# Twenty-eight tiles' experts chosen at the head of one step, the router's gap behind the k transposes, and one power of two columns

## The reference

```python
x = x + xattn(layernorm(x), ctx, ctx, Wq, bq, ..., Wo, bo)   # 16 heads of 32, 77 context tokens, causal mask
x = x + ffn(layernorm(x), ...)

# ffn(hidden), hidden read as S = 8, B = 512: attention runs over the 8 sequences
ln1 = layer_norm(hidden) * ln1_w + ln1_b
q, k, v = split(ln1 @ qkv.T)                   # 16 query heads, 4 k/v heads, causal over S
h1  = hidden + softmax(q k / sqrt(32)) v @ proj.T
ln2 = layer_norm(h1) * ln2_w + ln2_b
top_p, top_i = top_k(softmax(ln2 @ router), 2) # 8 experts, 2 per token, shares sum to 1
# tokens of each expert in order of their number, at most 1280 per expert
fc1 = gelu(tokens @ w1[e]);  fc2 = fc1 @ w2[e]
out = h1 + sum over the token's experts of share * fc2
```

## Time and profile before

| | us |
|---|---|
| median of 3 runs (lowest to highest) | 1679.21 (1679.16 to 1680.63) |
| profiled execution | 1678.78 |
| its span, first to last instruction | 1677.0 |
| PE busy in the span | 1520.7 (91%) |
| PEld, DVE, ACT, POOL busy | 1325.8, 951.9, 713.4, 837.0 |
| PE, DVE, POOL busy from 330 to 640 | 304.0, 226.5, 185.5 of 310 |
| PE, DVE, POOL busy from 850 to 900 | 21.9, 29.2, 11.8 of 50 |
| PE busy from 1000 to 1677 | 637.7 of 677 |

### The profile page before, as it was taken

The page is one execution under the profiler, slowest core; times in us unless marked ns, Lnnn a source line. Parts: engine busy times, 40 slices in busy tenths (PEclk is TensorE's granted clock), DMA queues, the critical chain, the costliest instruction groups (busy, mean ns, idle before and its releaser), DMA issues. The chain is left out here.

```text
span 1677.0 us, 30921 instructions
## 1 busy us (share of the span) xinstructions
PE 1520.7 (91%) x11103; PEld 1325.8 (79%) x11104; DVE 951.9 (57%) x1780; ACT 713.4 (43%) x1448; POOL 837.0 (50%) x953
## 2 busy tenths in 40 slices
PE   7788788999999999998863999899999979999986
PEld 5566677888888888877752989899999869899975
DVE  4766656777777767677756445543233555343361
ACT  2343443555554455455435434433332534343341
POOL 1343444556655556678741637453343665463242
PEclk9999889999999999999975999999999989999999
DMA  6111211122222212222211424343442533442221
GB/s 240 39 51 58 70 51 51 46 76 77 71 67 67 66 63 72 69 95 79 80 57 55 102 57 105 75 110 68 90 89 41 110 98 76 97 102 51 36 40 23
DMA packets 63597, 124.58 MB, mean 74 GB/s; under 512 B 13232, under 2 KB 13648, under 8 KB 62921
## 3 DMA queue, kind: packets, MB, share of 16 engines
q1 hardware_dynamic: 45184, 92.54, 16.9%
q0 software_dynamic: 17920, 29.31, 10.4%
q10 hardware_dynamic: 328, 0.50, 0.1%
HBM read 89.02 MB, written 46.27 MB: 81 GB/s over the span
## 5 line engine op out<-in xcount | busy, mean ns | idle before, releaser
L1351 PEld LDWEIGHTS hidden_ps<-gT,w 128*128 128x128 f32 x2880 | 350.4, 192 | 9.1 <-ACT hT L1270 4.2
L1351 PE MATMUL hidden_ps<-gT,w 128*128 128x256 f32 x2880 | 352.7, 284 | 5.3 <-ACT hT L1270 3.2
L1380 PE MATMUL expert_ps<-w,hT 128*128 128x512 f32 x1440 | 341.7, 397 | 8.1 <-DVE og L1320 8.1
L1380 PEld LDWEIGHTS expert_ps<-w,hT 128*128 128x128 f32 x1440 | 272.4, 191 | 65.9 <-DVE og L1320 8.5
L1295 DVE TENSOR_TENSOR hT<-gl,hT 128x512 fp32r<-128x512 f32 x160 | 130.5, 824 | 250.4 <-ACT hT L1270 250.3
L1155 POOL TENSOR_TENSOR w<-raw,w 128x1024 fp32r<-128x1024 f32 x64 | 155.0, 2433 | 201.2 <-ACT w L1149 200.8
L1268 ACT ACTIVATE gl<-hidden_ps 128x512 f32<-128x512 f32 x160 | 95.7, 598 | 335.3 <-PE hidden_ps L1351 312.6
L1252 POOL DMA_INDIRECT out_dram<-og,idx x80 | 130.3, 1628 | 153.7 <-DVE og L1320 140.0
L1320 DVE TENSOR_SCALAR og<-expert_ps,kept 128x512 f32<-128x512 f32 x80 | 59.1, 749 | 159.0 <-PE expert_ps L1380 154.9
L1278 ACT ACTIVATE gT<-yk 128x256 fp32r<-128x256 f32 x160 | 66.9, 418 | 109.1 <-DVE yk L1306 107.3
L1024 PE MATMUL main_ps<-wqkv_hi,zT 128*128 128x512 f32 x256 | 109.0, 441 | 4.8 <-DVE h L798 4.8
(11 more groups left out here) (178 smaller groups left out, 3225.6 us busy)
## 6 DMA issues: line engine op xcount, KB each, us to landing
raw<-L_ffn_moe_w_dram SPq DMA_DIRECT2D x64, 512.0 KB, 3.6
normed_tokens<-h SPq DMA_DIRECT2D x128, 65.0 KB
xa<-x_dram SPq DMA_DIRECT2D x32, 256.0 KB, 2.7
xc<-x_dram SPq DMA_DIRECT2D x32, 256.0 KB, 3.0
attended_rows<-x SPq DMA_DIRECT2D x32, 256.0 KB, 2.0
fx<-attended_rows SPq DMA_DIRECT2D x128, 64.0 KB
out_dram<-fx SPq DMA_DIRECT2D x128, 64.0 KB
fx<-qkv_rows_dram SPq DMA_DIRECT2D x1, 1536.0 KB, 6.6
```

The costliest lines, as they stand in the source:

```text
L1351: last = pe.matmul(pH[:, q, f * W:(f + 1) * W], w1[p][l][:, k, cols], xT[g.s % 2][r][:, k, :], start=k == 0 and n == 0, stop=k == KT - 1 a ...
L1380: last = pe.matmul(pY[:, k, :], hT[par][l][:, f, k * P:(k + 1) * P], w2[p][r][:, f, :], start=f == 0 and n == 0, stop=f == FT - 1 and n == 2)
```

## The change

- `CHOICES` has three batches: 28 tiles at step 48, 3 at step 50, the last one behind the loop. A batch is now chosen at the head of its step, ahead of the h addition. The buffer `equal` grows for it.
- MAX8 and gap stand behind the q and k transposes.
- `rff` goes. POOL makes both variances in two columns, one `pow` of two columns gives z's factor and h's, and `rstd_f` comes with that.
- The first expert's pieces are loaded at steps 38, 40, 42, 44, 46, 47, 48 and 49 (`FIRST_PIECES`) and halved one step later.
- `BY_ACT` is 4: VectorE makes four of the eight one-hot rows.
- ScalarE makes `wq_hi` ahead of its four first DMA issues, and the token tables and `wo_hi` in step 2 instead of step 1.

```diff
@@ -51,7 +51,7 @@
 BATCH = 8
-BY_ACT = 6
+BY_ACT = 4
@@ -162,8 +162,9 @@
 LATE = NT + LP + 2
-CHOICES = ((LATE, 0, 9), (LATE + 2, 9, 18), (LATE + 6, 18, 24), (LATE + 10, 24, 28), (STEPS - 2, 28, 31),
-           (STEPS, 31, 32))
+FIRST_PIECES = {LATE: (0,), LATE + 2: (1,), LATE + 4: (2,), LATE + 6: (3,), LATE + 8: (4,), LATE + 9: (5,),
+                LATE + 10: (6,), LATE + 11: (7,)}
+CHOICES = ((STEPS - 4, 0, 28), (STEPS - 2, 28, 31), (STEPS, 31, 32))
@@ -235,7 +236,7 @@
     token_mask = sb("token_mask", [TB, 16 * TB], F32R)
-    expo = sb("expo", [P, 1])
+    expo = sb("expo", [P, 2])
@@ -273,7 +274,7 @@
     wx, wf, wh = sb("wx", [P, 1]), sb("wf", [P, 2]), sb("wh", [P, 1])
-    rx, rf, rff, rh = sb("rx", [P, 2]), sb("rf", [P, 8]), sb("rff", [P, 2]), sb("rh", [P, 2])
+    rx, rf, rh = sb("rx", [P, 2]), sb("rf", [P, 8, 2]), sb("rh", [P, 2])
@@ -421,9 +422,9 @@
                     sp.dma_start(choice["product"][:, 0:3 * P], a["routing_orders"]).then_inc(const_in, 16)
-                if 0 <= i - LATE < CH:
+                for j in FIRST_PIECES.get(i, ()):
                     sp.wait_ge(s["x2_done"], NT)
-                    weights["load"](sp, 0, 0, 0, i - LATE)
+                    weights["load"](sp, 0, 0, 0, j)
@@ -504,13 +505,12 @@
                     var = mvf[:, f % 2, 1:2]
-                    link(pool, "pool_link", linked,
-                         pool.tensor_scalar(wf[:, 0:1], var, 1.0 + EPS, EPS * EPS, ALU.mult, ALU.add))
-                    pool.tensor_tensor(rff[:, f % 2:f % 2 + 1], wf[:, 0:1], expo[:, 0:1], ALU.pow)\
-                        .then_inc(s["rstd_f"], 1)
+                    pool.tensor_scalar(wf[:, 0:1], var, 1.0 + EPS, EPS * EPS, ALU.mult, ALU.add)
+                    link(pool, "pool_link", linked, pool.tensor_scalar(wf[:, 1:2], var, EPS, None, ALU.add))
                     need(pool, s["h0_done"], f - 7)
-                    link(pool, "pool_link", linked, power(rf[:, f % 8:f % 8 + 1], var, wf[:, 1:2]))
-                    pool.tensor_scalar(shift[:, f % 8:f % 8 + 1], mvf[:, f % 2, 0:1], rf[:, f % 8:f % 8 + 1], -1.0,
+                    pool.tensor_tensor(rf[:, f % 8, :], wf[:, :], expo[:, :], ALU.pow).then_inc(s["rstd_f"], 1)
+                    pool.wait_ge(s["rstd_f"], f + 1)
+                    pool.tensor_scalar(shift[:, f % 8:f % 8 + 1], mvf[:, f % 2, 0:1], rf[:, f % 8, 1:2], -1.0,
@@ -523,18 +523,18 @@
                     pool.memset(groups["xg"][:, :, :, :], 0.0).then_inc(s["xg_cleared"], 1)
-                if 0 <= i - LATE - 1 < CH:
-                    weights["low"](pool, 0, 0, i - LATE - 1)
+                for j in FIRST_PIECES.get(i - 1, ()):
+                    weights["low"](pool, 0, 0, j)
             pool.wait_ge(s["xg_cleared"], 1)
 
         @block.scalar
         def _(act):
+            act.wait_ge(wq_in, 16)
+            act.activation(wq[0][:, :, :], rq, ACT.Copy).then_inc(s["wq_hi"], 1)
             act.dma_start(x2[0:TB, 0, 0:P], a["token_sel"]).then_inc(tok_in, 16)
             act.dma_start(x2[0:TB, 1, :], a["token_mask"]).then_inc(tok_in, 16)
             act.dma_start(bv, a["L0_xattn_bv"].partition_broadcast(SK)).then_inc(bias_in, 16)
             act.dma_start(bo[:, :], a["L0_xattn_bo"].partition_broadcast(P)).then_inc(bias_in, 16)
-            act.wait_ge(wq_in, 16)
-            act.activation(wq[0][:, :, :], rq, ACT.Copy).then_inc(s["wq_hi"], 1)
@@ -542,7 +542,7 @@
                         .then_inc(s["xt_hi"], 1)
-                if i == 1:
+                if i == 2:
@@ -588,7 +588,7 @@
                     need(act, s["piece_lo"], 8)
                     act.activation(h1[:, f % 4, 0:D], fx[:, f % FX, :], ACT.Identity, bias=shift[:, f % 8:f % 8 + 1],
-                                   scale=rf[:, f % 8:f % 8 + 1]).then_inc(s["h0_done"], 1)
+                                   scale=rf[:, f % 8, 1:2]).then_inc(s["h0_done"], 1)
@@ -640,8 +640,8 @@
                         .then_inc(s["consts_done"], 1)
-                if 0 <= i - LATE - 1 < CH:
-                    weights["high"](act, 0, 0, i - LATE - 1)
+                for j in FIRST_PIECES.get(i - 1, ()):
+                    weights["high"](act, 0, 0, j)
@@ -791,6 +791,9 @@
                     low_halves(i)
+                batch = chosen(i, 0)
+                if batch is not None:
+                    choose(*batch)
@@ -859,12 +862,6 @@
                     dve.reciprocal(rec2[:, f % 2, :], den2[:, :]).then_inc(s["rec2_done"], 1)
-                f = tile(i, FF + 5)
-                if f is not None:
-                    dve.wait_ge(s["lg_evac"], f + 1)
-                    chained(dve.max(tops[:, f, :], logits[:, f, :]))
-                    need(dve, s["gap_exp"], f)
-                    dve.tensor_tensor(gap[:, :], tops[:, f, 1:2], tops[:, f, 0:1], ALU.subtract).then_inc(s["gap"], 1)
@@ -883,6 +880,12 @@
                     k_turn.then_inc(s["k_turned"], 1)
+                f = tile(i, FF + 5)
+                if f is not None:
+                    dve.wait_ge(s["lg_evac"], f + 1)
+                    chained(dve.max(tops[:, f, :], logits[:, f, :]))
+                    need(dve, s["gap_exp"], f)
+                    dve.tensor_tensor(gap[:, :], tops[:, f, 1:2], tops[:, f, 0:1], ALU.subtract).then_inc(s["gap"], 1)
@@ -904,11 +907,8 @@
                     dve.wait_ge(s["val_mm"], S)
                     need(dve, s["zt_mm"], f)
-                    dve.tensor_scalar(z, fx[:, f % FX, :], mvf[:, f % 2, 0:1], rff[:, f % 2:f % 2 + 1],
+                    dve.tensor_scalar(z, fx[:, f % FX, :], mvf[:, f % 2, 0:1], rf[:, f % 8, 0:1],
                                       ALU.subtract, ALU.mult).then_inc(s["z_done"], 1)
-                batch = chosen(i, 0)
-                if batch is not None:
-                    choose(*batch)
@@ -1081,7 +1081,7 @@
                "is_blk": sb("is_blk", [P, 2, BATCH, NBLK], F16), "hot_blk": sb("hot_blk", [P, 2, BATCH, NBLK], F16),
-               "equal": sb("equal", [P, 9, E]), "hot": sb("hot", [P, 2, NT, E]), "rest": sb("rest", [P, NT, E]),
+               "equal": sb("equal", [P, NT, E]), "hot": sb("hot", [P, 2, NT, E]), "rest": sb("rest", [P, NT, E]),
```

## The result

The changed kernel takes 1716.54 us (median of 4 runs, 1711.17 to 1718.79); the kernel before, run beside it, 1679.92 us (1679.16 to 1681.22). The ratio is 1.0213, with a 95% interval of 1.0187 to 1.0238. Slower was forecast; the size, +17.6 us for a measured +36.6, was wrong, and the time lies outside the range of 1684 to 1711. A second set of five runs of the changed kernel gave 1715.43 us and 1.0206 (1.0188 to 1.0224).

A forecast was written before the change was run, and what follows sets the result against it. Bound: TensorE in full steps, a ring through z in late steps, then a chain without overlap. Sum 11.3 - 0.5 + 2.9 + 3.4 + 3.3 - 4.8 + 0 + 2 = +17.6 on 1678.8: forecast 1696 us, range 1684 to 1711.

The forecast's parts named there:

- Parts 1 and 2, full steps: Steps 20 to 32: late gap and two-column power delay z and xT_lo, +11.3 us; a vanished wait gives -0.5.
- Part 2, steps 13 to 18: Steps without a gap yet: the later power ends before VectorE comes to z, so 0 us.
- Part 3: Late steps: z's chain has no slack, +1.95 us a turn; +5.8 before step 38, -2.9 to 47, together +2.9.
- Clock: Late turns: each leaves TensorE a 2 us hole, after which its clock may be lower; +2 us (0 to 13).
- the clock rival: Lower TensorE clock returns in every late turn: nine of 1.5 us, +13.5 instead of +2, total 1708 us; chance 0.20.
- Part 4: Head of step 48: choosing 28 tiles overruns VectorE's idle time, operations blocked by POOL; +3.4 us (0.2 to 4).
- Part 5: Counts: 84 matmuls instead of 12 before the last tile's router matmul; +3.3 us (+1 to +6).
- Part 6: One-hots: four tables instead of six on ScalarE shorten each batch; -4.8 us (-5.5 to -3.5).
- Part 7: Start: earlier wq_hi and later wo_hi, but the third x tile still waits for the queue; 0 us (-2 to +1).
- The gain rival: POOL is not late for z, only good parts stay: stretch from 38 to 47 shrinks 16.5, total 1661 us; chance 0.10.

The follow-up runs named there:

- e_gap: Kernel before with only MAX8 and gap moved behind the q and k transposes: 1701.45 us, ratio 1.0153.
- e_pow_wait: Kernel before with the two-column power, and POOL multiplying pr only after z of the step before is done: 1683.68 us, ratio 1.0018.
- e_after_fill: Changed kernel with 14 identity transposes on TensorE ahead of its wait for z, from step 37 on: 1705.7 us, ratio 1.0147.
- e_choices: Kernel before with only the new plan of choice batches and weight pieces: 1669.61 us, ratio 0.995.
- e_best4: Kernel before with the change minus moved gap and two-column power, fifth weight piece at step 45, 18 identity transposes before z2's wait, steps 47-49: 1661.42 us.

## Why the prediction was wrong

By its own terms, for the profiled execution (+32.1 us in the span, +17.6 forecast):

- **Parts 1 and 2, full steps: mechanism right, term too small.** 10.8 net forecast, 15.1 measured from step 19 to 33. 14 steps are longer, not 13, by 1.07 us on average and not 0.87. The step length follows xT_lo, and z comes 6.32 us behind `rec`'s start instead of 5.01, later by 1.31, not by the 1.14 worked out: 0.10 from L508 to the power, 0.05 in MAX8 to gap, the rest in single hundredths. Of it the gap alone makes 0.73 (e_gap), the power on top of it 0.34.
- **Part 2, steps 13 to 18: "0" failed.** 4.3 us from the 11th x addition on, and some 0.5 in the step ahead of it. I asked whether the power would be late, and it isn't. I did not ask what the removed power had kept back: POOL reaches its multiplication of pr 0.7 us sooner (1.60 instead of 2.29 behind L508) and meets z. The rows stood in the trace: in before z started at 315.47 and POOL's multiplication at 316.10. The earlier trace rows had shown what such a meeting costs, and I used it for part 4 alone. e_pow_wait shows the cause.
- **Part 3: the turns right, the clock not.** The three turns ahead of step 38 were +5.8 forecast; the four intervals from step 34 on are +5.2 in e_after_fill, and +8.1 in the changed kernel. The stretch from 38 to 47 was 126.5 forecast; it is 126.9 in e_after_fill and 133.5 in the changed kernel.
- **Clock: the step that failed by most.** +2 forecast, 9.5 us by e_after_fill in the profiled run; the late turns of the second profile are 2.4 us longer still. That is the clock rival's mechanism (forecast at +13.5 for nine turns), to which I gave 0.20; its count of nine was too high (five turns), its 1.5 a turn measured 1.3 in three and 2.8 and 3.0 in two. My reason against it, that 0.8 us holes in full steps show nothing, said nothing of holes of 2.66 us, and the earlier trace rows had just such a spell.
- **Part 4: +3.4 forecast, +2.9 measured** from 47 to 49, with the blocked operations as forecast (1.25 and 2.01 instead of 0.39). The rule of the Trainium skill (SBUF — State Buffer, "Who interferes with whom") asks for these, and the trace agrees.
- **Part 5: +3.3 and +3.3. Part 6: -4.8 and -4.7.** The counts run at the lower clock for 3.4 us, till 905.9.
- **Part 7: 0 forecast.** The first x addition came 1.8 us earlier, but in kernels without the moved copies it lies between 77.88 and 81.15 us, in those with them between 76.89 and 78.78. The means are 79.1 and 77.6, but the two ranges overlap: a gain of some 1.5 us isn't excluded, and isn't shown.

The power of two columns takes 0.72 us, one of one column 0.56. The rule of the Trainium skill (GPSIMD Engine Reference, section 3.1), which made a second column all but free, is off by 0.15 us for this operation.

The measured terms add up: -1.6 (up to the 11th x addition), +4.3, +15.1, +8.1, +4.1, +2.9, +3.3, -4.7, and 0.6 in the experts, 32.1. The median stands 5.4 us above the profiled execution; the second profile has 2.4 us of such a difference in the late turns and 2.2 in the expert part; the rest stays open.

The gain rival was wrong for this change and right for its other half: without the late gap the stretch shrinks by 16.0 us (e_choices), where it had said 16.5.

## What to carry to other kernels

A small operation that is moved "behind work that it does not depend on" has to be followed through the in-order queues of the engines that wait for it, to the end: here 0.3 us of VectorE's work, moved behind the transposes, cost 22 us alone and 43 beside a plan that had taken away what covered it. A removed operation also lets its engine arrive earlier at the next one: look for what that meets. Price parts in the schedule that the other parts leave, not in the old one, and where a ring gets a hole on TensorE, ask in every turn what its clock will do after it.

## What the runs showed of the hardware

- TensorE's clock after a hole: of the eight turns of steps 37 to 44, each behind a wait of 2.5 to 2.7 us for z, five lost time to the lower clock, 1.3 us in three and 2.8 and 3.0 in two. In the second profile it was partly other turns. Fourteen needless transposes in the hole kept the clock at 1.00 in all of them and made the kernel 10 us faster. In step 48 of e_best4, 18 of them (2.16 us) did so although 2.32 us of waiting were left behind them; in step 49, with 2.21 us left, the clock was 0.50 again from 0.5 us behind the wait on, for 3.3 us.
- POOL's power on 128 partitions takes 0.56 us for one column and 0.72 for two.
- VectorE's tensor_scalar on 512 elements takes 0.54 us alone and 1.45 when POOL's 128x616 multiplication starts 0.06 us before it; where POOL starts 0.56 us after it (528.95, in the full step shown), it keeps its 0.55.
